# First stage of a two-layer attention kernel: small VectorE work moved ahead of the units, every second sum moved from GpSimd to VectorE, fewer unread products

## The reference

```
x  [1024, 256];  xn = layernorm(x)
q = xn @ Wq (512 columns), k = xn @ Wk (128), v = xn @ Wv (128)
q, k rotated pairwise:  o1 = x1*cos - x2*sin,  o2 = x1*sin + x2*cos
two causal softmax maps per head, 16 heads:  a1 - lam * a2, with
lam = exp(sum(lambda_q1*lambda_k1)) - exp(sum(lambda_q2*lambda_k2)) + 0.2
s = groupnorm((a1 - lam*a2) @ v) @ Wo
g = silu(mxfp4(xn) @ mxfp4(W).T + bias)
x = x + s * g
then layer 1: plain causal attention times a routed mixture of experts
```

## Time and profile before

| | |
|---|---|
| median of three runs | 804.95 us |
| profiled execution | 807.48 us, its span 805.7 us |
| TensorE busy | 760.0 us (94%) |
| VectorE, ScalarE, GpSimd busy | 557.5, 425.8, 367.6 us |
| first block | to about 57.7 us |
| mean granted TensorE clock | 0.987 of full |

### The profile page before, as it was taken

One profiled execution on the slowest core, in us unless ns is written; L12 is line 12 of the kernel. 1 busy time (PEld: TensorE's weight loads), 2 busy tenths in 40 slices (PEclk: granted clock), 3 DMA queues, 4 the chain that ended last, 5 costly groups with the idle time before them and its releaser, 6 DMA issues. The chain is left out here.

```text
span 805.7 us, 12968 instructions
## 1 busy us (share of the span) xinstructions
PE 760.0 (94%) x3778; PEld 369.8 (46%) x3783; DVE 557.5 (69%) x1417; ACT 425.8 (53%) x915; POOL 367.6 (46%) x704
## 2 busy tenths in 40 slices
PE   4888999999999999999898899999899999999995
PEld 3342222222222223223655333332378888888883
DVE  3778777777777777723865878887277666566666
ACT  2432466666666666674233356767645553555552
POOL 1761566674234423441232133335356665566664
PEclk9999899999999999999999999999999999999998
DMA  6393641020011001102037254444442122221221
GB/s 200 118 291 116 158 109 35 18 67 16 15 39 49 19 16 43 41 22 61 0 120 198 80 149 112 162 157 137 136 116 69 64 64 55 53 66 58 67 69 55
DMA packets 56980, 68.86 MB, mean 85 GB/s; under 512 B 13793, under 2 KB 35714, under 8 KB 56915
## 3 DMA queue, kind: packets, MB, share of 16 engines
q1 hardware_dynamic: 56840, 68.10, 29.6%
q10 hardware_dynamic: 80, 0.07, 0.0%
HBM read 46.37 MB, written 15.44 MB: 77 GB/s over the span
## 5 line engine op out<-in xcount | busy, mean ns | idle before, releaser
L845 ACT ACTIVATE top<-ps 128x512 f32<-128x512 f32 (+3 forms) x384 | 170.7, 491 | 127.3 <-PE ps L764 127.2
L764 PE MATMUL ps<-mid 99*128 99x512 bf16 (+3 forms) x576 | 182.6, 332 | 4.1 <-ACT mid L845 2.5
L879 DVE CUSTOM_DVE_ANT_0 ps<-ps,keep 128x512 f32<-128x512 f32 (+3 forms) x320 | 162.0, 530 | 28.0 <-PE ps L740 27.8
L740 PE MATMUL ps<-mid 96*128 96x512 bf16 (+3 forms) x512 | 167.4, 340 | 5.5 <-PEq L249 1.4
L784 PE MATMUL ps<-top,mid 128*33 128x512 f32 (+3 forms) x768 | 162.6, 503 | 0.0
L1694 PE MATMUL ps<-xp,wp 128*128 128x512 f32 (+1 forms) x600 | 144.9, 390 | 1.3 <-DVE mid L1864 0.8
L764 PEld LDWEIGHTS ps<-mid 99*128 99x128 bf16 x576 | 53.6, 97 | 172.9 <-ACT top L845 103.2
L1694 PEld LDWEIGHTS ps<-xp,wp 128*128 128x128 f32 (+1 forms) x600 | 111.7, 187 | 26.3 <-issue 1.6
L979 POOL TENSOR_SCALAR_AFFINE_SELECT top<-top 128x128 f32<-128x128 f32 x256 | 71.7, 294 | 106.7 <-ACT top L845 104.7
L845 ACT ACTIVATE mid<-ps 128x512 f32<-128x512 f32 (+1 forms) x192 | 82.1, 493 | 55.2 <-PE ps L764 34.3
L883 DVE TENSOR_REDUCE top<-ps 128x1 f32<-128x512 f32 x128 | 88.4, 690 | 32.8 <-PE ps L740 32.2
(11 more groups left out here) (221 smaller groups left out, 849.7 us busy)
## 6 DMA issues: line engine op xcount, KB each, us to landing
mid<-part_scratch SPq DMA_DIRECT2D x9, 1152.0 KB, 8.7
part_scratch<-top SPq DMA_DIRECT2D x18, 384.0 KB, 3.0
mid<-combine_rows SPq DMA_DIRECT2D x48, 128.0 KB, 3.1
part_scratch<-top SPq DMA_DIRECT2D x18, 256.0 KB, 3.1
top<-in_w SPq DMA_DIRECT2D x6, 634.0 KB, 4.8
mid<-part_scratch SPq DMA_DIRECT2D x9, 384.0 KB, 4.0
top<-in_w SPq DMA_DIRECT2D x4, 640.0 KB, 7.3
top<-in_w SPq DMA_DIRECT2D x4, 633.0 KB, 5.4
```

The source lines that it names most:

```text
L740: nc.tensor.matmul(ps[:, s_bank(turn), 0:w], queries(pair, m)[0:PARTS, i * P:(i + 1) * P], keys(pair, m)[0:PARTS, c * 512:c * 512 + w], st ...
L764: nc.tensor.matmul(ps[:, ST_BANK + n % AHEAD, 0:w], keys(pair, m)[0:STACK, j * P:(j + 1) * P], queries(pair, m)[0:STACK, q0:q0 + w], start ...
L845: nc.scalar.activation(pr[:, n % RING, 0:w], ps[:, ST_BANK + n % AHEAD, 0:w], ACT.Exp, scale=0.25).then_inc(p_ready, 1)
L879: ins = nc.vector.tensor_tensor_reduce(bank, bank, msk[:, 512 - w:512], -1.0 if low else 1.0, 3e38 if low else -3e38, ALU.add, ALU.min if ...
```

## The change

Four edits, all in the first block. The seven bias parts, the copy of the mask and the sums of the lambdas leave the units and stand ahead of unit 0 on VectorE, behind one wait for all the small constants (`ld_c`). The sum `tA + tB` of units 1, 3, 5, 7 and 9 is formed by VectorE right behind its two products instead of by GpSimd; units 0, 2, 4, 6 and 8 stay where they were, and the semaphore `added` becomes one for each parity. The unread products behind v are 8 instead of 18.

```diff
@@ gpsimd
-                        if u < len(UN):
+                        if u < len(UN) and u % 2 == 0:
                             pool.wait_ge(roped, u + 1)
                             if u >= 2:
                                 pool.wait_ge(r1_ok, u - 1)
                             nc.gpsimd.tensor_tensor(qf[:, u % 2, :], tA[:, u % 2, :], tB[:, u % 2, :],
-                                                    ALU.add).then_inc(added, 1)
+                                                    ALU.add).then_inc(added[0], 1)
@@ scalar
-                            act.wait_ge(added, u + 1)
+                            act.wait_ge(added[u % 2], u // 2 + 1)
@@ vector
+                    dve.wait_ge(ld_c, 112)
+                    nc.vector.tensor_copy(msk[:, 384:512], tri[:, :])
+                    for n in range(2):
+                        last = nc.vector.tensor_tensor(lp[:, n, :], lm[:, 2 * n, :], lm[:, 2 * n + 1, :], ALU.mult)
+                    link(last)
+                    nc.vector.tensor_reduce(ls[:, :], lp[:, :, :], AX.X, ALU.add).then_inc(lsum, 1)
+                    for n in range(7):
+                        bias_part(n)
                     for u in range(len(UN) + 1):
                         if u < len(UN):
...
-                                dve.wait_ge(added, u - 1)
+                                dve.wait_ge(added[u % 2], u // 2)
...
-                        if u == 4:
...
+                            if u % 2 == 1:
+                                dve.wait_ge(roped, u + 1)
+                                if u >= 2:
+                                    dve.wait_ge(r1_ok, u - 1)
+                                nc.vector.tensor_tensor(qf[:, 1, :], tA[:, 1, :], tB[:, 1, :], ALU.add).then_inc(added[1], 1)
...
-                        if u >= 3:
-                            bias_part(u - 3)
@@ tensor
                     pe.wait_ge(roped, 8)
-                    for _ in range(18):
+                    for _ in range(8):
                         keep_busy(2)
```

More of the change, by code:

```diff
@@ L241, in program @@
             stats, rstd, normed, ids = (sem(n, a) for n in ("stats", "rstd", "normed", "ids"))
-            x_tr, xT_ok, proj, roped, added = (sem(n, a) for n in ("x_tr", "xT_ok", "proj", "roped", "added"))
+            x_tr, xT_ok, proj, roped = (sem(n, a) for n in ("x_tr", "xT_ok", "proj", "roped"))
+            added = [sem(f"added{n}", a) for n in range(2)]
             q_mm, qs_ok = sem("q_mm", a), sem("qs_ok", a)
```

## The result

The changed kernel took 806.85 us (median of 19 runs, 805.26 to 807.96) against 805.36 us for the kernel before on the same chip (19 runs, 803.70 to 808.04). The ratio is 1.0018, 95% interval 1.0010 to 1.0027: slower by 0.8 to 2.2 us. Forecast was 804.3, a small gain.

What follows compares the result with a forecast made beforehand. The prediction took a full DMA queue holding up SP's last writes to bound the first block. -1.9 us at the barrier and +1.3 in the opening gave -0.6, 804.95 to 804.3 us; eight times in ten 801.6 to 807.0.

Steps and rivals of the forecast that it cites:

- who bounds the block: End of first block: SP is last, its final writes held up by a full DMA queue, issue ending near 55.4.
- +1.3 in the opening: Second block's opening: 3.9 us at half clock after TensorE's stand makes the eight maxima steps lose 1.3 us.
- the bound, 1.8: Second block's opening: loss of the eight maxima steps if half clock lasts until the first score, 1.8 us.
- -1.9 at the barrier: Barrier between the blocks: DMA stretch and SP's last issue end sooner, second block opens 1.9 us sooner; bounds 0 and 5.1.
- cover for the early part: Ahead of unit 0: VectorE idles 6.92 us, 12.54 to 19.46, where the eleven instructions, 2.5 us, would fit.
- I take 0: Start of unit 0: constants land at about 15.7, early part ends at 18.2, delay 0; range 0 to 2.1 us.
- The fourth rival: Ahead of unit 0: constants land at 19.1, unit 0 starts 2.1 us later, kernel takes 806.25 us; chance 0.08.
- the sums are free: Odd units: the moved sum costs VectorE about what its subtraction does, 0.7 us.
- No slower than the even ones: Units of the first block: odd units, with sums on VectorE, are no slower than even ones, 5.9 us for two units.
- the 5.9: Units of the first block: two units take 5.9 us, where the last five before went at 7.0 for two.
- The sum: Whole kernel: -1.9 at the barrier and +1.3 in the opening give -0.6 us, 804.95 becoming 804.3.
- The third: Second block's opening: half clock lasts through nine unread products, opening loses 3.7 us, kernel takes 806.75 us; chance 0.15.

Runs made afterwards that it cites:

- kernel without products: The kernel before without any unread product behind v and without the wait ahead of them: 806.97 us against 804.31, ratio 1.0032.
- one more semaphore: The kernel before with one more semaphore that nothing uses: 805.16 us against 804.49, ratio 1.0012.
- cut alone: The kernel before with 8 unread products behind v instead of 18, nothing else: 805.3 us against 804.32, ratio 1.0018.
- 26 products: The changed kernel with 26 unread products instead of 8: 804.68 us against 804.32 for the kernel before, ratio 1.0002.
- odd sums alone: The kernel before with only the odd units' sums moved to VectorE, 18 unread products: 805.68 us against 804.49, ratio 1.0017.
- kernel with the late gather: The changed kernel with 16 unread products and the keys' large gather issued in the second block behind unit 9's write: 803.91 us against 804.32, ratio 0.9998.

## Why the prediction was wrong, by its steps

**Right: who bounds the block.** SP's last three writes were again long (6.56 us), its issue ended at 55.93 where 55.4 was forecast, the DMA share was near 1 from 42 on, SP's end followed unit 4's write (14.7 us behind 41.20, 14.8 behind 42.55 before), and units two apart were 6.15 where 5.9 was forecast. TensorE's stand (5.57) and the half clock were forecast too. The direction was lost in the sizes of the terms of the sum.

**Wrong: "+1.3 in the opening".** It measured 2.0 (11.15 less 9.18). The step that failed is taking 3.9 us of half clock from one earlier fall. (Even there the rows give 3.4, from 46.84 to 50.24; 3.9 counts from when the work came back.) The clock went down at about 56, still in the stand, and came back at 62.8, 6.2 us behind the opening, so all eight steps ran at half rate; I had worked that out as the bound, 1.8, and taken the smaller. The kernel without products shows the same 62.8 and 1.9.

**Wrong, and by most: "-1.9 at the barrier".** It measured -1.43 between the two traces, and about -0.3 in the mean of several. Traces with before's units opened at 57.99, 56.20 (8 products), 56.76 (none) and 57.35 (one more semaphore), mean 57.1; traces of the changed units at 56.56, 57.26 and 56.71, mean 56.8. The trace the prediction read was the latest of its kind: TensorE's first four records of `L431` stood 0.7 to 0.9 us apart in it, against 0.43 later, and unit 0 came at 19.46, where the other runs of before's units had it at 17.91 to 18.85. I read its wait of 6.92 us as cover for the early part. In the four other runs the cover ends 1 us sooner in the mean. In the cut alone, with before's units, unit 4's write was issued at 41.40, just 0.2 us behind the changed kernel's 41.20, and its block opened sooner (56.20). With 26 products, where the clock plays no part, the ratio of 1.0002 says the same.

**Wrong: "I take 0" for unit 0.** The landing was derived from `in_fw`, issued later; but the bias row itself was what VectorE waited for, until 16.85 to 17.64 in the six traces that have the early part behind constants in their old order. With 2.7 us of work unit 0 stood at 19.6 to 20.3, 0.5 to 2.0 behind the end of its swapped product. The fourth rival (constants at 19.1) had the mechanism; its landing was too late by 1.5 to 2.3 us.

**Wrong: the sums are free.** "No slower than the even ones" left out that GpSimd then has two subtractions in a row, which hold up VectorE's own. The prediction spoke of VectorE's sum meeting `lo` and did not put it into the sum; the sum took 0.91, it is the subtraction behind it that went from 0.68 to 1.64. (The copy in the earlier trace rows has one SBUF input. With two, before's `L404` took 1.43 at 33.53, beside GpSimd's subtraction, which had begun ahead of it, and 0.68 at 36.40, where it was itself ahead of the sum at 36.56.) It costs 0.27 us per two units (6.15 less 5.88). The working of the 5.9 has a slip as well: 1.86, 1.46, 1.26 and two times 0.58 are 5.7, and 6.1 only with 1.65 for the sum. From unit 6 to unit 8 the terms measured 2.08, 1.35, 1.65 and 1.08.

**The sum again.** Barrier -0.3, opening +2.0 in the executions in which the clock falls there (in how many it does, no trace of one execution tells), outside the span +0.35, where the prediction kept 1.78: +2.0 at most, against a measured 0.8 to 2.2.

**A rival that came near by luck.** The third, with 0.15, gave 806.75, and 806.85 was measured. But the clock was full again at 62.8, 3.0 us ahead of the nine unread products (65.77), so the opening lost 2.0 and not 3.7; what made up the number is the barrier, which gave less, and the time outside the span.

## What to carry to other kernels

Before shortening work ahead of a barrier, ask what the idle engine does to the opening of the next stage: here 18 unread products, 3.9 us of no use, brought back 1.3 us, and the whole rearrangement of the units, with the clock cured, nothing. Count such filler from the new end of the last engine, not in proportion to what was saved. And take a wait that is to serve as cover from several traces: its far edge is another engine's start, and moved by 1.5 us from run to run. The same holds for spans: behind the first score the 14 traces took 734.8 us (1.6 us of it at half clock) to 741.9 (14.7), more than anything that this change moves, so a span of one execution decides nothing here.

## What the runs showed of the hardware

- TensorE's first fp32 products of a kernel ran at half pace for a time that differs from run to run, while the granted clock is shown as 1.00: records 0.85 us apart up to 15.5 in the kernel before, 0.43 from the second on in the cut alone, from the first on in the odd sums alone. Of the 1.55 us between unit 0 at 17.91 there and at 19.46 before, all but the 0.14 by which TensorE started later go with this.
- Stand of TensorE ahead of the second block against the granted clock in its opening: in the nine traces with a stand of 0.45 to 2.03 us the clock held, as it did in the one with 3.14; in those with 3.50 and 3.54 half clock lasted 3.4 us, in those with 4.66 and 5.57 it lasted 6.8. The length of one stand doesn't tell alone: in the kernel before the clock also fell at 46.84, in work that came back behind a stand of 2.29 us.
- SP's issue of one write took 0.36 to 0.63 us for unit 6 of the kernel with the late gather, at a DMA share over 1, and 3.23, 2.29 and 0.96 us for unit 7 of the changed kernel, right behind the large gather.
- Seven loads issued by ScalarE at the same time as SP's, 0.30 MB together, delayed the first part of x by 1.6 us and the identity by 4.5.
